# AdaLN block with top-2 experts on one core: in layer two of the experts the activations stand and the weights are streamed

## The reference, cut to what matters

```python
logits = silu(x @ rw1 + rb1) @ rw2 + rb2
k_logits, k_index = top_k(logits, 2)
k_prob = softmax(k_logits)
for e in range(8):
    we = sum(where(k_index == e, k_prob, 0.0), axis=-1)
    h = silu(x @ w1[e] + b1[e]) @ w2[e] + b2[e]      # 128 -> 512 -> 128
    out = out + we[:, None] * h
x = x + gb * out
```

## Time and profile before

| | |
|---|---|
| timed runs, median (lowest to highest) | 313.73 us (313.26 to 314.92) |
| profiled execution, span from first to last instruction | 344.7 us |
| TensorE, mean granted clock | 0.880 of full speed |
| busy: PE / PEld / DVE / ACT / POOL | 273.9 / 208.6 / 196.8 / 172.6 / 164.5 us |
| chain that ended last, by engine | PE 58%; DVE 14%; another core or an unknown queue 9%; ACT 8%; issue 5% |

### The profile page before, as it was taken

How to read it: one execution, slowest core, us unless ns; L and a number is a source line. 1 busy time by engine, 2 the same in 40 slices (tenths; PEclk the granted TensorE clock), 3 DMA queues, 4 the chain that set the end, 5 groups by cost and what they waited for, 6 DMA issues and landing times.

```text
span 344.7 us, 5139 instructions
## 1 busy us (share of the span) xinstructions
PE 273.9 (79%) x1290; PEld 208.6 (61%) x1290; DVE 196.8 (57%) x730; ACT 172.6 (50%) x327; POOL 164.5 (48%) x181
## 2 busy tenths in 40 slices
PE   0877598996978856999934799999999999999400
PEld 0543246664546444868823578888888888888300
DVE  4989899876967643544450234444434444447626
ACT  1079988796867403532400444555555554555100
POOL 4322013378668471547575344544555445555700
PEclk9999698788797876986996699999999999999955
DMA  8990000011111151101122353222222365002366
GB/s 232 321 276 0 0 2 2 8 57 39 40 46 42 54 142 29 33 32 54 42 77 77 92 136 96 70 60 55 62 72 76 84 172 156 19 23 67 92 186 179
DMA packets 41080, 28.43 MB, mean 82 GB/s; under 512 B 4895, under 2 KB 37713, under 8 KB 41056
## 3 DMA queue, kind: packets, MB, share of 16 engines
q1 hardware_dynamic: 34034, 18.60, 20.1%
q0 software_dynamic: 4544, 8.47, 7.5%
q10 hardware_dynamic: 2478, 1.09, 1.2%
HBM read 16.39 MB, written 12.67 MB: 84 GB/s over the span
## 4 chain that ended last, share of the span: by engine, by line
PE 58%; DVE 14%; another core or an unknown queue 9%; ACT 8%; issue 5%; DMA 3%; POOL 1%; DVEq 1%; SPq 0%; POOLq 0%; ACTq 0%
PE bank L1052 20%; PE bank L1065 16%; PE bank L1001 7%; PE bank L1015 4%; PE bank L1041 3%; PE bank L1073 2%; PE bank L977 2%; PE bank L930 2%; PE bank L978 2%; DVE st L630 2%; DMA av<-expert_out 1%; ACT hT L525 1%; ACT hT L585 1%; DVE rows L725 1%
## 5 line engine op out<-in xcount | busy, mean ns | idle before, releaser
L492 POOL DMA_INDIRECT expert_out<-shared,tx x78 | 78.0, 1000 | 73.1 <-DVE shared L890 59.7
L585 ACT ACTIVATE hT<-bank,w_t 128x256 f32<-128x256 f32 x156 | 65.2, 471 | 45.5 <-PE bank L1052 26.1
L483 POOL DMA_INDIRECT sorted_rows<-rows,sloti x64 | 65.3, 1021 | 41.4 <-DVE sloti L769 23.8
L1052 PE MATMUL bank<-xT,w_t 128*128 128x256 f32 x312 | 79.8, 402 | 0.0
L1065 PE MATMUL bank<-hT,w_t 128*128 128x256 f32 x312 | 75.8, 387 | 0.1
L1052 PEld LDWEIGHTS bank<-xT,w_t 128*128 128x128 f32 x312 | 60.8, 204 | 8.9 <-issue 1.2
L1065 PEld LDWEIGHTS bank<-hT,w_t 128*128 128x128 f32 x312 | 57.8, 196 | 6.8 <-DVE w_t L882 0.3
L1001 PE MATMUL bank<-h2T,rw_s 128*128 128x512 f32 x64 | 41.5, 752 | 7.8 <-issue 3.9
L594 ACT ACTIVATE yT<-bank,w_t 128x256 f32<-128x256 f32 x39 | 18.5, 474 | 49.9 <-PE bank L1065 32.0
L864 DVE COPY xT<-bank 128x256 f32<-128x256 f32 x39 | 16.5, 424 | 39.3 <-PE bank L1041 21.8
L873 DVE COPY w_t<-w_s 128x516 f32 x39 | 17.2, 440 | 25.0 <-issue 13.9
(11 more groups left out here) (176 smaller groups left out, 354.6 us busy)
## 6 DMA issues: line engine op xcount, KB each, us to landing
tx<-sorted_rows SPq DMA_DIRECT2D x39, 130.0 KB
w_s<-in_L_ffn_w_dram SPq DMA_DIRECT2D x16, 256.0 KB, 6.2
xs<-in_L_attn_x_dram SPq DMA_DIRECT2D x8, 256.0 KB, 5.2
av<-expert_out SPq DMA_DIRECT2D x8, 256.0 KB, 3.8
qv<-expert_out SPq DMA_DIRECT2D x8, 256.0 KB, 5.4
expert_out<-shared,tx POOLq DMA_INDIRECT x78
sorted_rows<-padr SPq DMA_DIRECT2D x9, 130.0 KB
sorted_rows<-rows,sloti POOLq DMA_INDIRECT x64
```

The lines of the kernel that those rows point to most:

```text
L483: p.indirect_dma_start(sorted_rows[:, :], bass.IndirectOffsetOnAxis(ap=sloti[:, k, t:t + 1], axis=0), rows[:, t, k, :], None).then_inc(s_d ...
L492: p.indirect_dma_start(expert_out[:, :], bass.IndirectOffsetOnAxis(ap=xr_i[:, s % U, n, D + 1:D + 2], axis=0), yo[:, s % U, n, :], None, b ...
L585: ins = nc.scalar.activation(hsT[:, u % 2, h, :], bank[4 + q][:, (h % 2) * SL:(h % 2 + 1) * SL], ACT.Silu, bias=w1_t[:, u % 2, HID + h:HID ...
L1052: ins = t.matmul(bank[4 + h // 2][:, (h % 2) * SL:(h % 2 + 1) * SL], w1_t[:, u % 2, h * P:(h + 1) * P], xT[:, u % 2, :], start=True, stop= ...
```

## The change: what it does

Layer two swaps its operands. The stationary operand is now a 128x128 piece of the activations `hsT` (128 rows of the tile, 128 hidden features), the moving operand the matching 128 columns of `w2_t`. Two halves of the tile by four pieces make 8 products of 128 columns, where there were 4 of 256. The result has the tile's rows on the partitions, so `turn_out` and its two transposes go, and bank 1 serves `tx` alone. `bias_out` on ScalarE goes too. In their place VectorE runs `add_bias` (plan name `ad`): the bias row is added to bank 7 into the new tile `yb`, and a second instruction multiplies `yb` by the shares. For this the bias must stand as a row on all partitions: `b2` is loaded by one DMA that writes it to 128 partitions behind the weights in `w2_s`, and `w2_t` is 640 wide and no longer 513. The turned bias columns of `b2`, their DMA on ScalarE's queue and their copy go.

TensorE's step `s` becomes `tx` of s+1, `l1` of s, `l2` of s-1; VectorE's becomes `ad` of s-2, then `xT` and `w1` of s+1, `w2` of s, `combine`. All four strings of `PLAN` are new, from the first stage on, the steps of the groups included.

```diff
-    W2E = HC * D + 1
+    W2E = HC * D + D
-        b2_c = smallbT[:, NSB - NE:NSB].unsqueeze(2)
-        yT = sb("yT", [P, 2, SL])
+        yb = sb("yb", [P, 2, HALVES, D])
...
 "tensor" of PLAN, from before the last logits to tile 9:
-  logits:7 tx:4 l1:3 ty:1 l2:2 rank:7 tx:5 l1:4 ty:2 l2:3 tx:6 l1:5 ty:3 count:1 l2:4 tx:7 l1:6 ty:4
-  l2:5 tx:8 l1:7 ty:5 l2:6 l1:8 ty:6 l2:7 tx:9
+  logits:7 tx:5 l1:4 rank:7 tx:6 l2:3 tx:7 count:1 l1:5 l1:6 l2:4 l2:5 tx:8 l1:7 l2:6 l1:8 l2:7 tx:9
 "vector", its start:
-  stats1:0 setup:0 norm1:0 setup2:0 soft:0 colsb:0 mods:0 stats1:1
+  setup:0 stats1:0 colsb:0 stats1:1 setup2:0 norm1:0 soft:0 mods:0
 "scalar", an example:
-  tanh:1 decay:1 clamp:1 modulate:3 tanh:2 decay:2 tanh:3 decay:3 mult:1
+  tanh:1 decay:1 tanh:2 tanh:3 decay:2 decay:3 clamp:1 mult:1
...
+            sp.dma_start(w2_s[:, :].rearrange("p (e w) -> p e w", e=NE)[:, :, HC * D:W2E],
+                         b2.unsqueeze(0).to_broadcast([P, NE, D])).then_inc(s_w2, 16)
...
-            act.dma_start(smallb[NSB - NE:NSB, :], b2).then_inc(s_smallb, 16)
...
-            def bias_out(s, u):
-                act.wait_ge(s_l2, s + 1)
-                if not (static(s) and s < 2):
-                    act.wait_ge(s_yturn, s - 1)
-                nc.scalar.activation(yT[:, u % 2, :], bank[7][:, 0:SL], ACT.Identity,
-                                     bias=w2_t[:, u % 2, HC * D:W2E]).then_inc(s_yT_e, 1)
...
-            def scale_y(s, u):
-                dve.wait_ge(s_yturn, s + 1)
+            def add_bias(s, u):
+                dve.wait_ge(s_l2, s + 1)
...
-                v.tensor_tensor(yo[:, u, :, :], bank[1][:, 0:SL].rearrange("p (n d) -> p n d", n=HALVES),
+                v.tensor_tensor(yb[:, u % 2, :, :], bank[7][:, 0:SL].rearrange("p (n d) -> p n d", n=HALVES),
+                                w2_t[:, u % 2, HC * D:W2E].unsqueeze(1).to_broadcast([P, HALVES, D]),
+                                ALU.add).then_inc(s_yb, 1)
+                dve.wait_ge(s_yb, s + 1)
+                v.tensor_tensor(yo[:, u, :, :], yb[:, u % 2, :, :],
                                 xr[:, u, :, D:D + 1].to_broadcast([P, HALVES, D]), ALU.mult).then_inc(s_yo, 1)
...
             def layer2(s, u):
...
-                    pe.wait_ge(s_yT_e, s)
-                for h in range(HC):
-                    ins = t.matmul(bank[7][:, 0:SL], w2_t[:, u % 2, h * D:(h + 1) * D], hsT[:, u % 2, h, :],
-                                   start=(h == 0), stop=(h == HC - 1))
+                    pe.wait_ge(s_yb, s)
+                for n in range(HALVES):
+                    for h in range(HC):
+                        ins = t.matmul(bank[7][:, n * D:(n + 1) * D], hsT[:, u % 2, h, n * P:(n + 1) * P],
+                                       w2_t[:, u % 2, h * D:(h + 1) * D], start=(h == 0), stop=(h == HC - 1))
                 ins.then_inc(s_l2, 1)
-
-            def turn_out(s, u):
-                pe.wait_ge(s_yT_e, s + 1)
-                wait_tile_bank(pe, "ty", s)
-                for n in range(HALVES):
-                    ins = t.transpose(bank[1][:, n * P:(n + 1) * P], yT[:, u % 2, n * P:(n + 1) * P], ident[:, :])
-                ins.then_inc(s_yturn, 1)
```

More of the change, by code:

```diff
@@ L234, in adaln_block @@
             "tensor": """
[L235 to L239, removed]
@@ L245, in adaln_block @@
-                ty:9 l2:10""",
-            "vector": """
[L247 to L255, removed]
@@ new lines, in adaln_block @@
+                gates:3 turn_y:0 turn_x:4 turn_x:5 turn_y:1 turn_h:0 gates:4 turn_y:2 turn_y:3 router:0
+                router:1 router:2 gates:5 turn_h:1 router:3 router:4 turn_x:6 router:5 logits:0 turn_h:2
+                router:6 rank:0 router:7 router:8 router:9 logits:1 router:10 router:11 turn_h:3 rank:1
+                gates:6 turn_y:4 logits:2 turn_y:5 turn_x:7 router:12 router:13 router:14 router:15 gates:7
+                rank:2 logits:3 turn_h:4 turn_h:5 router:16 turn_y:6 rank:3 router:17 router:18 router:19
@@ new lines, in adaln_block @@
+                turn_y:7 router:20 count:0 router:21 logits:4 turn_h:6 router:22 router:23 router:24 rank:4
+                router:25 router:26 router:27 logits:5 tx:0 tx:1 l1:0 tx:2 l1:1 rank:5 turn_h:7 l2:0 logits:6
+                router:28 tx:3 router:29 l1:2 rank:6 l2:1 tx:4 router:30 router:31 l1:3 l2:2 logits:7 tx:5
+                l1:4 rank:7 tx:6 l2:3 tx:7 count:1 l1:5 l1:6 l2:4 l2:5 tx:8 l1:7 l2:6 l1:8 l2:7 tx:9 tx:10
+                l1:9 tx:11 l2:8 l1:10 l2:9 tx:12 l1:11 l2:10""",
@@ new lines, in adaln_block @@
+            "vector": """
+                setup:0 stats1:0 colsb:0 stats1:1 setup2:0 norm1:0 soft:0 mods:0 stats1:2 csilb:0 norm1:1
+                stats1:3 norm1:2 stats1:4 stats1:5 norm1:3 stats1:6 input:0 scan:0 rowsA:0 input:1 input:2
+                input:3 resid:0 norm1:4 norm1:5 norm2:0 scan:1 scan:2 scan:3 resid:1 norm1:6 norm2:1 resid:2
+                resid:3 input:4 norm2:2 consts:0 top2:0 stats1:7 place:0 norm2:3 norm1:7 top2:1 input:5 scan:4
+                scan:5 place:1 resid:4 resid:5 top2:2 input:6 norm2:4 norm2:5 place:2 top2:3 input:7 scan:6
+                scan:7 resid:6 place:3 resid:7 norm2:6 top2:4 place:4 table1:0 w2:0 w2:1 norm2:7 w1:0 w1:1
+                xT:0 top2:5 xT:1 xT:2 place:5 w1:2 rowsB:0 table1b:0 ad:0 top2:6 place:6 xT:3 w2:2 w1:3 w1:4
+                xT:4 ad:1 ad:2 w2:3 w1:5 top2:7 xT:5 w2:4 w1:6 place:7 xT:6 ad:3 table2:0 w2:5 ad:4 w1:7 xT:7
+                w1:8 xT:8 w2:6 ad:5 ad:6 w2:7 w2:8 w1:9 w1:10 xT:9 xT:10 ad:7 w2:9 ad:8 w1:11 w1:12 xT:11
+                xT:12 w2:10 ad:9 w2:11""",
@@ L1038, in turn_rows @@
                 pe.wait_ge(s_xr[u], 16 * rounds(s, u))
-                wait_tile_bank(pe, "tx", s)
+                if static(s) and s == 0:
+                    wait_tile_bank(pe, "tx", s)
+                else:
+                    pe.wait_ge(s_xT, s)
                 for n in range(HALVES):
```

89 lines of the change are left out of this document (33 added, 56 removed).

## The result

| | before | after |
|---|---|---|
| timed runs of one session, median (lowest to highest) | 314.28 us (313.26 to 314.92) | 319.76 us (318.91 to 320.96) |
| ratio | | 1.018, interval 1.014 to 1.021 |
| profiled execution (before: that of r1): time, span | 313.97, 312.1 us | 319.54, 317.7 us |
| busy: PE / DVE / ACT / POOL | 265.0 / 196.2 / 172.8 / 165.0 us | 260.6 / 211.7 / 151.7 / 168.6 us |

The prediction was 308.5 us, with a range of 304.0 to 312.6; the kernel moved the other way. Executions of one kernel scatter by 1.5 to 6 us (the kernel before: 310.2 to 316.4 over all sessions; one of r5's four took 410.3 us), so a single profiled execution can stand 3 us off its median.

A forecast was written before the change was run, and what follows sets the result against it. The prediction took PE to bound every tile it has data for, at 3.90 us a tile. From 313.7 us, -4.2 (tiles 9 to 34), -1.3 (up to tile 9) and +0.3 (last tiles) gave 308.5 us, range 304.0 to 312.6.

The forecast's parts named there:

- Layer two on PE: Each tile's layer two: 16 load-and-matmul pairs at 0.112 us, 1.79 us in place of 1.95, a gain of 0.16 us.
- who waits in the loop: Loop: no engine but PE holds it; DVE's step 3.0 us of a 3.74 us period, ACT, GpSimd and `b2` DMA cost nothing.
- tiles 9 to 34: Loop tiles paid by PE alone: 26 x 0.16 = 4.2 us gained (3.4 to 4.9).
- rival C: Every layer two: the load is not hidden behind 128 columns, so the kernel is slower, about 335 us; chance 0.08.
- rival D: Loop: DVE becomes the bound, with a step of 4.1 us the kernel takes 319 us; chance 0.06.
- The prediction's terms for VectorE's step: VectorE's loop step: addition, wait, product, `xT`, `w1` and `w2` with register reads, summed by the prediction to 3.0 us.
- the estimate that the prediction drew from the Trainium skill: Layer two: load only partly hidden, ratio 1.45 on 0.11, so 0.16 us a pair and 2.55 us instead of 1.79.
- The last tiles: From step 36, combining makes DVE set the end; the tail gives 0.2 to 0.3 us back.
- Up to tile 9: Before tile 9: `count:1` comes 2.15 us earlier, 0.8 given back, 1.3 us gained; the loads set `tx:9` both times.
- The first stage: Start: fewer ACT table loads against a first modulation 3.4 us later; costed at 0, ends 3.4 loss and 3 gain.
- one of the signs of being wrong that the prediction named: Signs: pitch over 0.122 us, loop clock under 1.00, PE waiting for `yb`, or `count:1` and first `router` later than before.
- Rival B: Late first modulation carried to the end, +3.4, plus stalls of `l1` and `l2` pairs (0.2 + 0.5): 312.6 us; chance 0.18.

The follow-up runs named there:

- r1: The kernel before, unchanged, profiled once more: 314.0 us, ratio 0.998, span 312.1 us.
- r5: r4 with `mult:4` right behind `clamp:4` on ScalarE and `scan:4` right behind `place:0` on VectorE: 327.1 us, ratio 1.043.
- r9: New product, all lists cut once at 80 to 90 us, old orders ahead and new orders behind: 322.1 us, ratio 1.024 to the kernel before.
- r13: r9 with `silu:12`, `silu:13` and `copy:4` moved earlier on ScalarE and `router:16` ahead of `turn_h:5` on TensorE: 317.2 us, ratio 1.012.
- r8: New product, all lists cut once at 80 to 90 us, new orders ahead and old orders behind: 324.2 us, ratio 1.030 to the kernel before.
- r10: New product, new orders only up to about 48 us, the old order behind that: 318.5 us, ratio 1.013 to the kernel before.
- r6: The kernel before with `dup:0` and `dup:1` moved behind `silu:9` on ScalarE: 320.5 us, ratio 1.022.
- r4: The changed kernel with `dup:0` moved from behind `silu:9` to right behind `silu:4` on ScalarE: 319.7 us, ratio 1.021 to the kernel before.
- r14: The changed kernel with the edits of r4 and r13, plus `turn_h:4` ahead of `logits:3` and `router:12` ahead of `turn_y:5` and `turn_x:7`: 320.8 us, ratio 1.026.

## Why the prediction was wrong

**Layer two on PE, who waits in the loop, tiles 9 to 34: right.** 1.79 us for a layer two forecast, 1.78 measured; 4.2 us for the 26 tiles forecast, 3.8 measured (0.17 a period in the loop, less in the first three tiles, which wait for loads). The recorded load is 192 ns long and costs next to nothing: no rival C. VectorE never holds the loop: no rival D; the 640-column copy takes 0.495 us, 0.50 forecast. (The prediction's terms for VectorE's step add up to 2.65 us, not the 3.0 that it gives; from the addition's start to the end of `w2` it measures 2.8, from 262.39 to 265.15.) By the estimate that the prediction drew from the Trainium skill, "TensorE: Matmul & The Clock Gate", section "Back-to-back issue gap", layer two would have been 2.55 us; for fp32 products at the full clock the trace, with 1.78, disagrees.

**The last tiles: mechanism right, size off.** 0.2 to 0.3 us forecast, 0.7 measured. From the end of tile 34's layer two to the end of the last product my sum of VectorE's steps gave 16.9 us, and it took 17.4 (280.85 to 298.21); the first scatter of the last tile starts 17.7 us behind that event, 17.0 before. After, the end of the tail in VectorE's and GpSimd's rows, which answer:

```profile
297.78 0.43 DVE L869 TENSOR_TENSOR shared<-yb,tx 128x256 f32<-128x256 f32 x1
298.57 0.98 POOL L480 DMA_INDIRECT expert_out<-shared,tx  x1 [0.30 <-DVE shared L869]
299.85 0.98 POOL L480 DMA_INDIRECT expert_out<-shared,tx  x1 [0.30 <-issue]
```

and before (r1):

```profile
291.69 0.42 DVE L890 TENSOR_TENSOR shared<-bank,tx 128x256 f32<-128x256 f32 x1
292.93 0.98 POOL L492 DMA_INDIRECT expert_out<-shared,tx  x1 [0.30 <-issue]
294.22 0.98 POOL L492 DMA_INDIRECT expert_out<-shared,tx  x1 [0.30 <-issue]
```

Before, the last scatters waited for GpSimd's own queue (1.24 us from the start of the last product to the first of them); now it is 0.79, and the product itself is late.

**Up to tile 9: the step that failed**, forecast -1.3, measured +8.7. It said that `tx:9` "is set by the loads both times" and counted what stands on PE between `logits:7` and `count:1`. That count was right: from the start of `logits:7` to the count it is 9.9 us after (150.78 to 160.70) and was 15.3 (138.76 to 154.08). But `logits:7` itself starts 12.0 us later: 8.2 from `router:16`, and 3.8 for `tx:4`, `l1:3` and `l2:2`, which now stand ahead of it (0.22 + 1.73 + 1.78). From the count to tile 9 it is 15.3 us before and 17.4 after, where "about 15" stood for both: 12.0 - 5.4 + 2.1 = 8.7. Of the 2.1, 1.1 is PE's work that the prediction itself counted (14.3 against 13.2) and took for covered; the rest no run separates. Nor did the loads set tile 9 both times: in the kernel before (r1) PE began it straight behind a layer two, in the changed kernel it first sat idle for 0.56 us until the load landed:

```profile
169.40 0.38 PE L1041 MATMUL bank<-ident,tx 128*128 128x128 f32 x2
178.10 0.44 PE L1023 MATMUL bank<-ident,tx 128*128 128x128 f32 x2 [0.56 <-DMA tx<-sorted_rows]
```

The count and SyncE's queue after, which answer:

```profile
160.70 0.17 PE L1014 MATMUL bank<-mboth,ones_h 128*128 128x8 f16 x1
```

```profile
161.94 8.46 SPq L352 DMA_DIRECT2D sorted_rows<-padr  x8
174.07 7.12 SPq L363 DMA_DIRECT2D tx<-sorted_rows  x6
```

The mistake behind it is in the reading of the profile. I named the stretch from 125 to 207 us as disturbed and then argued from its gaps all the same: that PE had idle time there, so that only the loads counted. Undisturbed, PE is busy without a gap from 100 to 152, and what reaches it late at 90 us is late at the end, give or take what the clock does in between.

**The first stage: costed at 0 with ends of +3.4 and -3, and the other half of the failed step.** The first `modulate` is 2.1 us late (3.4 forecast) and the fourth scan 1.8 early ("about even"), both as argued; 16 table loads where I counted 15. But the router does not follow the fourth scan: its first step is 3.7 us late (46.9 against 43.2), one of the signs of being wrong that the prediction named, behind `gates:4`, `turn_y:2` and `turn_y:3` in PE's new list. And I followed only groups 0 to 3, whose router steps are 2.7 to 5.1 us late. The fifth group's steps in the same lists (`mult:4`, `copy:4`) and `dup:0`, which holds GpSimd up, I never placed in time. The +8.2 us at its first router step are nearly the whole of the 8.7. Rival B named a late start that is carried through, but priced the wrong one.

**What stays open.** The list behind the cut is shown as a cause by r9 and r13, the front by r8 and r10, with the reservation on cut lists; that `dup:0` can do it is shown in the old orders (r6), not in the new ones (r4). r14 was to undo both and left the fifth scan late, so no run brings the new orders to 89 us at `router:16`, and how the front's 7.8 us split beyond the 4.5 of the first 48 us was not measured. Nor is it known what moves the granted clock between 0.82 and 0.89 in the stretch behind `router:16`, which makes up to some 7 us of difference between runs.

## What to carry to other kernels

When a change comes with new orders, find the point from which the bound engine has hardly a gap, and follow every list to that point, for the group that reaches it, not for the first ones. Two late chains that meet at one step don't add: undoing one shows nothing, so cut the lists in halves before you undo single steps. A gain in a product and a plan are separate changes: here the product in the old orders, with the freed addition kept off the table's queue and the combining moved behind the tiles, gives 311.2 us (ratio 0.993) where the whole change gives 319.8 (1.018). And read TensorE's granted clock beside the length of every stretch in which it is the bound, before a step is credited with the difference.
